# A recurrent attention block on one core: banks used twice in a section, queries read where they lie, roots as powers, and another order

## What is computed

```
xx = shift(x) - x                                   # x is first layer-normed
mix = tanh((x + xx*maa_x) @ w1) ;  four blends xrg, xwa, xk, xv = x + xx*(maa + mix_i)
r = xrg@wr ; k = xk@wk ; v = xv@wv ; g = tanh(xrg@g1)@g2
w = -softplus(-(decay + tanh(xwa@wd1)@wd2)) - 0.5   # log of the decay
kk = normalised over each head (k + tanh(xk@kk1)@kk2) ; a, ma, mk2 = sigmoids of low-rank terms
S_t = S_{t-1}*diag(exp(w_t)) + (S_{t-1} a_t) b_t^T + v_t k_t^T ;  y_t = S_t r_t
y = groupnorm(y)*ln_w + ln_b + (sum r*k*faaaa) * v ;  attn = (y * g) @ w_output
ffn = silu( (silu(x@wg) * (x@wu)) @ wd ) ;  out = x + ffn * attn
```

## Time and profile before

| | |
|---|---|
| median of 3 runs | 1800.61 us |
| profiled execution | 1809.13 us, span 1807.7 us |
| granted TensorE clock, mean | 0.941 |
| busy: PE / DVE / ACT / POOL | 90% / 68% / 67% / 27% |
| chain that ended last | PE 77%, SP's queue 6%, DVE 5%, ACT 4%, DMA 4%, issue 3% |
| DMA | 57.83 MB, mean 32 GB/s |

### The profile page before, as it was taken

How to read it: one execution, slowest core, us unless ns; L and a number is a source line. 1 busy time by engine, 2 the same in 40 slices (tenths; PEclk the granted TensorE clock), 3 DMA queues, 4 the chain that set the end, 5 groups by cost and what they waited for, 6 DMA issues and landing times.

```text
span 1807.7 us, 47903 instructions
## 1 busy us (share of the span) xinstructions
PE 1625.3 (90%) x20224; PEld 1116.4 (62%) x20224; DVE 1234.1 (68%) x2608; ACT 1207.0 (67%) x2047; POOL 480.0 (27%) x388
## 2 busy tenths in 40 slices
PE   1679999999998999999899999999999999999966
PEld 0255757667575766757576675757667575765745
DVE  3476777677676777767677676777777676776713
ACT  1838758584875858587584958768585875849512
POOL 0414132241313224141332414132241413324000
PEclk9879999999998999999899999999999999999968
DMA  3011020211202021110201112030211203011110
GB/s 132 12 17 31 9 51 14 50 22 30 42 8 51 14 46 25 30 42 6 54 15 40 31 30 42 3 58 14 45 26 30 42 3 58 14 40 19 35 25 25
DMA packets 251430, 57.83 MB, mean 32 GB/s; under 512 B 223696, under 2 KB 250704, under 8 KB 251088
## 3 DMA queue, kind: packets, MB, share of 16 engines
q1 hardware_dynamic: 241936, 41.95, 12.3%
q10 hardware_dynamic: 9280, 12.81, 2.0%
HBM read 36.38 MB, written 18.35 MB: 30 GB/s over the span
## 4 chain that ended last, share of the span: by engine, by line
PE 77%; SPq 6%; DVE 5%; ACT 4%; DMA 4%; issue 3%; POOL 0%; DVEq 0%; ACTq 0%
PE bank L356 16%; PE bank L506 16%; PE bank L516 10%; PE bank L481 7%; DMA Y<-in_x 3%; PE chunk L612 3%; PE chunk L584 3%; PE chunk L559 3%; PE bank L455 3%; PE chunk L568 2%; PE bank L468 2%; PE bank L634 2%; PE bank L461 2%; PE chunk L598 2%; SPq L1342 1%
## 5 line engine op out<-in xcount | busy, mean ns | idle before, releaser
L506 PE MATMUL bank<-xT,wu 128*128 128x256 f32 x768 | 219.8, 423 | 0.0
L506 PE MATMUL bank<-xT,wg 128*128 128x256 f32 x768 | 202.1, 400 | 18.3 <-DVE KS L962 18.3
L1305 POOL TENSOR_TENSOR SF<-ST,CT 128x256 f32<-128x256 f32 x128 | 97.4, 761 | 450.4 <-DVE ST L1168 450.4
L839 ACT ACTIVATE sg<-bank 128x512 f32<-128x512 f32 x96 | 57.1, 595 | 228.9 <-PE bank L506 228.5
L516 PE MATMUL bank<-wd,hT 128*128 128x256 f32 x768 | 186.5, 393 | 0.0
L1246 POOL TENSOR_TENSOR big<-KS,xT 128x512 f32<-128x512 f32 x64 | 75.2, 1197 | 407.1 <-DVE KS L962 407.1
L506 PEld LDWEIGHTS bank<-xT,wg 128*128 128x128 f32 x768 | 142.8, 196 | 60.1 <-DVE KS L962 30.7
L356 PE MATMUL bank<-big,W 128*128 128x512 f32 (+1 forms) x320 | 167.2, 657 | 13.1 <-POOL big L1246 6.5
L506 PEld LDWEIGHTS bank<-xT,wu 128*128 128x128 f32 x768 | 151.3, 209 | 36.6 <-issue 11.4
L516 PEld LDWEIGHTS bank<-wd,hT 128*128 128x128 f32 x768 | 143.2, 193 | 22.0
L356 PE MATMUL bank<-KS,W 128*128 128x512 f32 x320 | 144.2, 597 | 0.0
(11 more groups left out here) (161 smaller groups left out, 3559.9 us busy)
## 6 DMA issues: line engine op xcount, KB each, us to landing
smalls<-in_x SPq DMA_DIRECT2D x32, 256.0 KB, 3.0
Y<-in_x SPq DMA_DIRECT2D x32, 256.0 KB, 3.7
out<-fsil ACTq DMA_DIRECT2D x32, 256.0 KB, 2.2
scrA<-AM SPq DMA_DIRECT2D x64, 64.0 KB, 1.9
hat<-scrB SPq DMA_DIRECT2D x32, 128.0 KB, 3.3
hat<-scrF SPq DMA_DIRECT2D x32, 128.0 KB, 3.1
KE<-scrA SPq DMA_DIRECT2D x64, 32.0 KB, 2.3
scrT<-KE SPq DMA_DIRECT2D x16, 128.0 KB, 1.7
```

The costliest lines, as they stand in the source:

```text
L506: q = pe.matmul(o[:, TT_ * n2:TT_ * n2 + TT_], w[:, h, 128 * (n + n2):128 * (n + n2) + 128], x_now[:, h], start=(h == 0), stop=(h == NH - 1))
L839: act.activation(sg[:, :], ring.tile(key)[:, :], ACT.Silu).then_inc(*sg_ready.up)
L1305: pool.tensor_tensor(SF[:, :, :, :], ST[:, :, :, :], fade[:, c].unsqueeze(3).to_broadcast([128, B, NH, N]), ALU.mult).then_inc(*faded.up)
```

## The change

It has four parts.

1. **A second ring.** The recurrence's four banks become a ring of their own, `spare`, and `early_room` takes from it. `mix0`, `lora`, `z`, `na0`, `nma0`, `k0`, `k1`, `hk`, `gh`, `r0`, `r1`, `v0` and `v1` go there. The recurrence waits until all of them have been read.
2. **Queries from their tile.** `qpad` and ScalarE's copies go. The two query tiles are one tile QQ, and each matmul of the pairs becomes two, one for each head: 64 rows of the array, 16 moving columns. Each head has its own bank, and VectorE makes two masked copies of 128x256 in place of one of 128x512.
3. **Roots as powers.** GpSimd adds epsilon and raises to -0.5, for both norms. ScalarE's square roots and VectorE's reciprocals go, and the factor 1/64 goes into the square before it.
4. **New order** strings for all four engines.

```diff
-ORDER = {"pe": ("NNNFNOONNNNOFNFNKOFRVKKVRRBBKVNNBBKVBVBBVBBBBBNBBBNBBBNBBNBBNEBNNNBBNNBBNNBNBBXXBBNXXXBXBBNBBLBNBBXX"
+ORDER = {"pe": ("NFNNNONONNNOFNNFKFOKKRVKRVNNRKBBVVVNNVBBBNBNBNBNBBEBBNBBNBBNBNBBBNBBNNBBNBBBXBXBBLBBXXBBXBBXBNBNBBXX"
             "BBLXXXX"),
-         "act": ("ONNNFKFFFOOFFRFDKVKDVBRRBKKKVVBEBKBBBKVBXXBBVDBVBBVNNXBLBBNXBNBBXXLBXBBLLBXBBNXBBLXX"),
-         "dve": ("BOFNOONBBBOBFFFFFFFBOBBBBBBBBBBBDDDDDKKDDNKDKDBBBXEBLBEXBXBEXBXEXENXXBXXLXBNXXBXXXXXNBXXXBXXXXXBXXXL"
-             "BLXXXBXBX"),
-         "pool": ("FFFFFFFFDBFEXEBKBXBBBBBL")}
+         "act": ("NNOFKNFFFFFFKDKDKVKVRKEBKBOVVRKRVVBVXBXNBVNBBDBBBXBBBNLBBBNBBBLXBBLBBBBXNBBLXX"),
+         "dve": ("BOFNOONBOFFFFFBFBFBBBOBBBBBBBBBBKDDDKNDKKDEDXDDEBDEBXLBNBEXXBXBXEXBXLXXBXXXNBXBXNXXBXXBXXXXBXXBXXXLL"
+             "XBXXXXBBX"),
+         "pool": ("FFFFFFFBFEFEDXKBXLBBLBBBBB")}
...
+            def early_room(t, key, emptied):
+                o, before = spare.take(key, emptied)
+                if before:
+                    pe.wait_ge(*before)
+                if t >= 2:
+                    pe.wait_ge(*y_out(t - 2))
+                    pe.wait_ge(*st_ready(t - 2))
+                return o
...
             def pairs(t):
+                queries = QQ[:, :, :, :].rearrange("p x h (q j e) -> p x (h q) j e", j=NJ, e=BL)
+                pe.wait_ge(*qa_ready(t))
+                pe.wait_ge(*qr_ready(t))
                 for qt in range(NK):
-                    K, Q, E = KSb[qt % 2], qpad[qt % 2], KE[qt % 2]
-                    o = room((t, "A", qt), am_ready(t, qt + 1))
-                    pe.wait_ge(*q_made(t, qt + 1))
+                    K, E = KSb[qt % 2], KE[qt % 2]
+                    two = [room((t, "A", qt, hh), am_ready(t, 2 * qt + hh + 1)) for hh in range(2)]
                     pe.wait_ge(*keys_made(t, qt + 1))
                     for n in range(QC // 2):
                         for j in range(NJ):
                             for b in range(B):
-                                oc = o[64 * b:64 * b + 64, 128 * n:128 * n + 128].rearrange("p (x e) -> p x e", e=L)
-                                q = pe.matmul(oc[:, :, BL * j:BL * j + BL], K[:, 2 * n + b, 64 * j:64 * j + 64],
-                                              Q[:, 2 * n + b, j, :, :, :].rearrange("p a b e -> p (a b) e"), start=True, stop=True)
+                                for hh, o in enumerate(two):
+                                    oc = o[64 * b:64 * b + 64, 64 * n:64 * n + 64].rearrange("p (x e) -> p x e", e=L)
+                                    q = pe.matmul(oc[:, :, BL * j:BL * j + BL], K[64 * hh:64 * hh + 64, 2 * n + b, 64 * j:64 * j + 64],
+                                                  queries[64 * hh:64 * hh + 64, :, QC * qt + 2 * n + b, j, :], start=True, stop=True)
+                                    if (n, j, b) == (QC // 2 - 1, NJ - 1, B - 1):
+                                        q.then_inc(*ring.fill((t, "A", qt, hh)))
...
                 if t + 1 < NT:
-                    for taken in (z_ready, na_ready, nma_ready):
-                        pe.wait_ge(*taken(t + 1, 2 if taken is z_ready else 1))
+                    for taken in (z_ready, k_ready, hk_ready, gh_ready, r_ready, v_ready):
+                        pe.wait_ge(*taken(t + 1))
+                    for taken in (na_ready, nma_ready):
+                        pe.wait_ge(*taken(t + 1, 1))
...
-                    for hh in range(2):
-                        p0 = 64 * hh
-                        for x, own in ((0, a5), (1, r5)):
-                            i = act.activation(Q[p0:p0 + 64, :, :, hh, x, :], own[p0:p0 + 64, qs], ACT.Copy)
...
-                act.activation(rstd[:, :], mv[:, :, 1], ACT.Sqrt, bias=eps[:, 0:1]).then_inc(*x_std.up)
-                act.activation(st2[:, :], st2[:, :], ACT.Sqrt, bias=eps[:, 1:2], scale=1.0 / N).then_inc(*y_std.up)
-                dve.reciprocal(rstd[:, :], rstd[:, :]).then_inc(*rstd_inv.up)
-                dve.reciprocal(st2[:, :], st2[:, :]).then_inc(*y_inv.up)
...
-                    dve.copy_predicated(AM[par][:, 4 * b:4 * b + 4, 128 * h:128 * h + 128].rearrange("p n (g c) -> p n g c", g=2),
+                    for hh in range(2):
+                        key = (t, "A", qt, hh)
+                        dve.wait_ge(*ring.full(key))
+                        dve.copy_predicated(AM[par][:, 4 * b:4 * b + 4, 128 * h + 64 * hh:128 * h + 64 * hh + 64],
...
+                pool.wait_ge(*mv_ready(t))
+                pool.tensor_scalar(rstd[:, :], mv[:, :, 1], LN_EPS, None, ALU.add).then_inc(*x_std.up)
+                pool.wait_ge(*x_std(t))
+                pool.tensor_tensor(rstd[:, :], rstd[:, :], minus_half.to_broadcast([128, NM]), ALU.pow).then_inc(*rstd_inv.up)
...
+                pool.wait_ge(*y_var(t))
+                pool.tensor_scalar(st2[:, :], st2[:, :], GN_EPS, None, ALU.add).then_inc(*y_std.up)
+                pool.wait_ge(*y_std(t))
+                pool.tensor_tensor(st2[:, :], st2[:, :], minus_half.to_broadcast([128, NM * H]), ALU.pow).then_inc(*y_inv.up)
```

More of the change, by code:

```diff
@@ L162, in program @@
         rstd, nmean = sb("rstd", [128, NM]), sb("nmean", [128, NM])
-        big = [sb(f"big{i}", [128, NH, COLS]) for i in range(4)]
+        big = [sb(f"big{i}", [128, NH, COLS]) for i in range(2)]
+        QQ = sb("QQ", [128, 2, NH, COLS])
         KB = sb("KB", [128, 2, NH, COLS])
@@ L169, in program @@
         KE = [KE2[:, i] for i in range(2)]
-        qpad = [sb(f"qpad{i}", [128, QC, NJ, 2, 2, BL]) for i in range(2)]
         duo = [k[:, :, :].rearrange("p q n -> p (q n)").rearrange("p (a h n) -> p a h n", a=2, h=NH) for k in KSb]
@@ L375, in mixing @@
                 pe.wait_ge(*mixh_ready(t))
-                if t >= 2:
-                    pe.wait_ge(*y_out(t - 2))
-                    pe.wait_ge(*st_ready(t - 2))
-                for n in range(4):
+                four = [early_room(t, (t, "mix0", n), mixed(t, 2 * n + 1)) for n in range(4)]
+                for n, o in enumerate(four):
                     f = MIX[n][0]
-                    pe.matmul(spare_bank[n], w2[32 * f:32 * f + 32, 0:128], small[32 * f:32 * f + 32, :], start=True, stop=True).then_inc(*mix_made.up)
+                    pe.matmul(o, w2[32 * f:32 * f + 32, 0:128], small[32 * f:32 * f + 32, :], start=True, stop=True).then_inc(*spare.fill((t, "mix0", n)))
                 yield "mix0"
@@ L405, in mixing @@
                     k = 32 - 32 * g
-                    pe.matmul(spare_bank[g], wa2[k:k + 32, 128 * g:128 * g + 128], sml2[k:k + 32, :], start=False, stop=True).then_inc(*z_made.up)
+                    pe.matmul(four[g], wa2[k:k + 32, 128 * g:128 * g + 128], sml2[k:k + 32, :], start=False, stop=True).then_inc(*spare.fill((t, "z", g)))
                 yield "z"
@@ L1241, in mixing @@
                 if t:
-                    pool.wait_ge(*q_made(t - 1))
+                    for hh in range(2):
+                        pool.wait_ge(*ring.full((t - 1, "A", NK - 1, hh)))
                 for k, (n, h) in enumerate(MIXED):
@@ L1252, in decays @@
             def decays(t):
-                pool.wait_ge(*ring.full((t, "v", NH - 1)))
+                pool.wait_ge(*spare.full((t, "v", NH - 1)))
                 pool.memset(FL[:, :, :], 0.0).then_inc(*fl_zero.up)
```

143 lines of the change are left out of this document (60 added, 83 removed).

## The result

The kernel after takes 1835.51 us (median of 4 runs, 1831.55 to 1841.53) against 1801.44 us for before on the same chip: a ratio of 1.018, 95% interval 1.014 to 1.023. It is slower; 1750 us, in a range of 1700 to 1808, was forecast. The profiled execution took 1831.55 us, 22.4 more than the one of before. The medians lie 34.1 us apart: before's profiled execution is the longest of its four, after's the shortest. So what follows from the two profiles accounts for 22.4 of some 34 us.

The account below looks back on a forecast made before the run. TensorE, 90% busy, was taken to bound the kernel through its work plus stalls, with clock loss second. Stalls -27, clock -18, start and tail -9, masked copies +3 make -51: 1800.6 to 1750 us, range 1700 to 1808.

Parts of the forecast that it names:

- the +3: End of a section: transfers wait for VectorE's last masked copy, 0.2 us x 16 = +3 us.
- the own banks mean that k1, hk, gh, v0, r0, v1 and r1 wait only for ScalarE to read what stood there two to four steps earlier: Second ring, steps behind `z`: they wait only for ScalarE, which has lost 9.7 us of work a section.
- I take the pairs at no change: Pairs on TensorE: 128 narrower matmuls on four quarters are 32 rounds again, so a group costs 0 us more.
- the first rival: Pairs: feeding TensorE becomes the bound, 26 ns a matmul, +86 us, 1836 us; chance 0.18, 0.15 of it slower.
- I take 18: Granted clock behind `corner`: denser work keeps it up more often, 18 of at most 25 us gained.
- 0.97 was the sign of being right: Steady stretch between first and last `band`: mean granted clock at 0.97 or more, from 0.96 before.
- The clock falls in the pairs, since fewer columns stream there: Pairs: a lower clock there, listed as a sign of being wrong, with no size given.
- half of the waits before `mix1` and that `gate` goes: TensorE's waits before `mix1` and the `gate` after it, 1.05 + 1.25 us a section: half goes, 1.15 us.
- The new place: ScalarE between `band` and `state0`, with `u0` directly behind: new waits of 0.4 + 0.2 us a section.
- The roots at nothing: Both norms' roots as powers on GpSimd: 0 us, with -3 to +10 us kept for the range.
- New waits take the place of the old ones: VectorE's and ScalarE's strict orders: stalls only move, the new place costs 1.5 us a section, 1788 us; chance 0.17.
- The third rival: Whole kernel: clock high nearly throughout and stalls nearly gone, 1800 - 40 - 50 = 1710 us; chance 0.10.

Follow-up runs that it names:

- e5: Before with part 1 alone, the second ring, in the old order with whole pairs: ratio 1.0121, 1825.1 us.
- e8: Before with parts 1 and 3, the second ring and the roots as powers, old order and whole pairs: ratio 1.0120, 1826.7 us.
- e2: After with part 2 alone undone, so whole pairs from qpad with ScalarE's copies: ratio 1.0133, 1826.9 us.
- e13: e5 with gh, the step behind z in the old order, moved to the first ring: ratio 1.0043, 1811.9 us.
- e4: After with z moved behind out1 and g1 moved between state0 and u0 in TensorE's order: ratio 1.0260, 1849.4 us.
- e14: e4 with k1, the step behind z there, moved to the first ring: ratio 1.0159, 1834.8 us.
- e17: e15 with k1 put back in the second ring, directly behind z: ratio 1.0214, 1843.6 us.
- e15: e14 with whole pairs instead of split ones: ratio 0.9913, 1797.5 us.
- e6: After with the second head's matmuls of the pairs left out but for each group's last: ratio 1.0153, 1830.5 us.

## Why the prediction was wrong

The ledger of the profiled executions: idle +19.5, active +1.6, start +5.0, tail -3.7, together +22.4 us where -51 was forecast. Of these 73 us some 43 lie in the stalls (-24 forecast, with the +3), 20 in the active time (-18 forecast) and 10 at the ends (-9 forecast). The runs that add one part after the other say where it went: the ring takes the ratio to 1.0121 (e5), the roots leave it at 1.0120 (e8), the order takes it to 1.0133 (e2) and the split pairs to 1.0184 (after).

- **The failed step: "the own banks mean that k1, hk, gh, v0, r0, v1 and r1 wait only for ScalarE to read what stood there two to four steps earlier".** I had counted one bank for each step. `z`, which takes four at once, is not in that list, and its wait had no term. It takes the bank filled by the step just ahead of it, and leaves to the step behind it a bank that ScalarE has still to read. That is 18.2 us over the 15 sections before `z` where I had 0, and it is most of the cost of the ring: e13, without it, is at 1.0043 where e5 is at 1.0121; e4 against e14 and e17 against e15 say the same. At 1.2 us a section it cancels the 18.9 us that the waits before `vT0` and `kk` gave back.
- **The second failed step: the pairs, "I take the pairs at no change".** The round was right: 2.06 us for 128 MATMULs, (2.06 - 0.214) / 127 = 14.5 ns each. The Trainium skill's floor of about 25 ns in "TensorE: Matmul & The Clock Gate" (Part 1) does not hold on four quarters of the array. But a group is not all: I had put at nothing, and left to the first rival, how fast the instructions themselves can come. 15.0 us of "issue" waits stand in the pairs and 10.7 elsewhere, most of it in `s`, `y` and `u` behind them. In the kernel as changed the split costs only 0.5%, hardly clear of noise, and whole pairs have the lower clock there (e2); with the other waits gone it costs 2.5% (e15 against e14): about 17 us of idle and 25 us of activity.
- **The third failed step: the clock, "I take 18".** The waits before `kk` and `vT0` went, and so did the low clock around `corner`, but it came back among the pairs: low time 116 to 133 us, and a mean of 0.95 where 0.97 was the sign of being right. By e2 against e8 the new order itself brings it, and with it go 25 us more of active time where I had a gain, as much as the 23 us of idle time that the order saves. "The clock falls in the pairs, since fewer columns stream there" stood among the signs of being wrong, without a price. That it falls there is right; the reason is not shown, since it falls there with whole pairs too. What doubled columns bring is 21 to 25 us in three comparisons.
- **Stalls.** That `kk` and `vT0` no longer wait is right (6.9 + 12.0 us over 15 sections), and the 8.7 us before `state` went too. That half of the waits before `mix1` and that `gate` goes is wrong: 29.9 us in the earlier trace rows, 29.7 now. (The forecast had divided these by 13 waits and the others by 14 sections, which makes a difference of 1 us.) The new place was forecast at 0.6 us a section, and `u` got 7.5 / 15 = 0.50; `s` got 5.3 us that nothing had foreseen.
- **The roots at nothing** is right, though a power lies above my upper end of 1.5 us for the larger tile:

```profile
L1300 POOL TENSOR_TENSOR st<-st,one 128x16 f32<-128x16 f32 x16 | 46.8, 2926 | 1.3
...
L1218 POOL TENSOR_TENSOR rstd<-rstd,one 128x4 f32<-128x4 f32 x16 | 17.6, 1103 | 1.3
```

- **ScalarE and VectorE** came out as worked out: three table loads a section fewer, 1052 us busy, and a masked copy of 256 columns at 439 ns (477 taken):

```profile
L831 ACT ACT_TABLE_LOAD x16 | 20.5, 1283 | 0.3
```

```profile
L1098 DVE COPY_PREDICATED AM<-mask,bank 128x256 f32<-128x256 uint32 x128 | 49.5, 439 | 25.6 <-PE bank L495 24.5
```

- **Start and tail**: +1.3 instead of -9.

Of the rivals, "feeding TensorE becomes the bound" named 1836 us, which is the measured time, by luck. Its MATMULs of 26 ns would have cost 86 us in all; they came at 14.5 ns, and the feed shows as 25.7 us of single stalls. "New waits take the place of the old ones" had the mechanism, but named another place (1788 us) and not `z`. The third rival's 1710 us does not follow from its own terms: 63 us of clock and 60% of 96 us are 121 us, not 90.

Open remain the loading of instructions as the cause of the "issue" waits, why the new order lets the clock fall among the pairs, the link from a wait to the clock 30 us later, the 12 us by which the medians differ more than the profiled executions, and 0.4% by which e13 is slower than before at the same idle time.

## What to carry to other kernels

Where banks are handed out in turn, write down for each step how many it takes at once, and who reads the bank that it gets: a step that takes the whole ring ties together the step ahead of it and the step behind it, and putting one neighbour into another ring undoes that. Splitting a matmul into row quarters took no more array time here but doubled the instructions; look for "issue" waits. Idle time taken out can come back as low clock: here a new order saved 23 us of waits and lost 25 us of active time, and a short wait cost between three quarters of its length and nearly three times it. So read the active time of TensorE and the granted clock beside the idle time before a gain or a cost is counted.

## What the hardware showed that I had not expected

- 128 MATMULs with their weight loads, on four quarters of the array, in 2.06 us, as long as 64 on two halves.
- TensorE stopping 0.5 to 1.8 us once or twice a section with no semaphore to wait for, in and behind stretches of 256 instructions in 2 us; next to none with half the instructions (1.3 us in all in e6).
- Doubling the columns of 8192 MATMULs, with no new result computed, made the kernel 21 to 25 us faster in three pairs of kernels, by the ratios.
- The order of steps alone moved the low clock from `corner` to the pairs and raised the low time from 98 to 156 us (e8, e2).
- A power on GpSimd: 2926 ns for 128x16, 1103 ns for 128x4.
